# Loads begun a stage earlier, a shorter tables chain, and an edge softmax on 128 partitions

## The reference

```
x += gnn0(norm(x))   # three layers: batch-norm over the nodes, gather of the edges' source rows,
                     # degree-weighted sum by target, product with W (512x512), relu
x += ffn0(norm(x))   # each of 32 experts takes its 312 best tokens; up (512x1365), silu, down
                     # (one up matrix serves 4 experts), scatter-add weighted with the router's share
x += gnn1(norm(x))   # attention along edges: logits = q[rows].k[cols]/8 + edge_attr (8 heads)
                     # row_max = segment_max(logits, rows); p = exp(logits - row_max[rows])
                     # att = p / segment_sum(p, rows)[rows]; y = segment_sum(att * v[cols], rows)
x += ffn1(norm(x))   # two experts of 8 for each token, 512x32 each, gelu
```

## Time and profile before

| | |
|---|---|
| median of three runs | 3903.74 us (3902.39 to 3907.45) |
| the profiled execution's own time | 3906.87 us |
| its span, first to last instruction | 3905.1 us |
| mean granted TensorE clock | 0.886 of full speed |
| TensorE matmuls busy | 3254.1 us, 83% of the span |
| VectorE busy | 2462.7 us, 63% |
| ScalarE busy | 1388.0 us, 36% |
| GpSimd busy | 1235.2 us, 32% |

### The profile page before, as it was taken

The page is one execution under the profiler, slowest core; times in us unless marked ns, Lnnn a source line. Parts: engine busy times, 40 slices in busy tenths (PEclk is TensorE's granted clock), DMA queues, the critical chain, the costliest instruction groups (busy, mean ns, idle before and its releaser), DMA issues. The chain is left out here.

```text
span 3905.1 us, 61914 instructions
## 1 busy us (share of the span) xinstructions
PE 3254.1 (83%) x18334; PEld 2750.4 (70%) x18335; DVE 2462.7 (63%) x5844; ACT 1388.0 (36%) x2580; POOL 1235.2 (32%) x1606
## 2 busy tenths in 40 slices
PE   6845889997775309999999999999679992969999
PEld 1213667776774209999999999999668881856766
DVE  7855877644766764545455444454278877957776
ACT  4633655421112314445444444444211111114443
POOL 4752532222551012323222322323123320025552
PEclk9977999997555559999999999999889995989999
DMA  4313323335994034544444444444322111146663
GB/s 157 99 24 105 106 94 122 100 124 167 305 306 135 0 76 113 133 116 136 126 111 137 102 133 143 99 137 113 66 64 59 54 43 42 67 122 149 161 155 104
DMA packets 250361, 449.60 MB, mean 115 GB/s; under 512 B 65632, under 2 KB 71073, under 8 KB 249591
## 3 DMA queue, kind: packets, MB, share of 16 engines
q1 hardware_dynamic: 176425, 280.66, 22.0%
q0 software_dynamic: 62368, 145.38, 17.1%
q10 hardware_dynamic: 11318, 20.54, 1.4%
HBM read 319.38 MB, written 126.83 MB: 114 GB/s over the span
## 5 line engine op out<-in xcount | busy, mean ns | idle before, releaser
L1460 PE MATMUL experts_psU<-experts_x_hi,experts_up_hi 128*128 128x312 f32 (+1 forms) x1408 | 443.3, 315 | 22.9 <-issue 16.5
L1489 PE MATMUL experts_psY<-experts_hid_hi,experts_dn_hi 128*128 128x312 f32 (+1 forms) x1408 | 439.0, 312 | 0.0
L1461 PE MATMUL experts_psU<-experts_x_lo,experts_up_hi 128*128 128x312 f32 (+1 forms) x1408 | 436.8, 310 | 0.0
L1462 PE MATMUL experts_psU<-experts_x_hi,experts_up_lo 128*128 128x312 f32 (+1 forms) x1408 | 435.6, 309 | 0.0
L1490 PE MATMUL experts_psY<-experts_hid_lo,experts_dn_hi 128*128 128x312 f32 (+1 forms) x1408 | 431.3, 306 | 0.0
L1491 PE MATMUL experts_psY<-experts_hid_hi,experts_dn_lo 128*128 128x312 f32 (+1 forms) x1408 | 429.7, 305 | 0.0
L1419 POOL DMA_INDIRECT experts_xg<-xn,experts_token_i x96 | 123.4, 1285 | 663.0 <-DVE experts_token_i L1586 643.5
L1625 DVE TENSOR_TENSOR experts_hid_lo<-experts_hid,experts_hid_hi 128x312 fp32r<-128x312 f32 (+1 forms) x352 | 161.2, 480 | 252.2 <-ACT experts_hid L1552 252.2
L1550 ACT ACTIVATE experts_hid_hi<-experts_psU,experts_bup 128x312 fp32r<-128x312 f32 (+1 forms) x352 | 183.6, 522 | 322.1 <-PE experts_psU L1462 320.3
L1460 PEld LDWEIGHTS experts_psU<-experts_x_hi,experts_up_hi 128*128 128x128 f32 (+1 forms) x1408 | 265.2, 188 | 24.4 <-issue 22.0
L1617 DVE TENSOR_TENSOR experts_dn_lo<-experts_dn_raw,experts_dn_hi 128x1536 fp32r<-128x1536 f32 (+1 forms) x128 | 208.0, 1625 | 98.6 <-ACT experts_dn_hi L1528 98.4
(11 more groups left out here) (412 smaller groups left out, 8158.7 us busy)
## 6 DMA issues: line engine op xcount, KB each, us to landing
experts_dn_raw<-in_L_ffn_W_down SPq DMA_DIRECT2D x96, 768.0 KB, 4.6
conv<-gcn_diff SPq DMA_DIRECT2D x120, 256.0 KB, 2.9
experts_up_raw<-in_L_ffn_W_up SPq DMA_DIRECT2D x32, 682.5 KB, 8.4
index_xt<-in_x SPq DMA_DIRECT2D x78, 256.0 KB, 2.8
route_xt<-in_x SPq DMA_DIRECT2D x78, 256.0 KB, 4.9
x<-route_xt SPq DMA_DIRECT2D x78, 256.0 KB, 4.3
xn<-route_xn ACTq DMA_DIRECT2D x78, 256.0 KB, 5.0
two_xt<-x SPq DMA_DIRECT2D x78, 256.0 KB, 2.8
```

The costliest lines, as they stand in the source:

```text
L1460: pe.matmul(acc, up_hi[:, c, cols], x_hi[:, c, :], start=(c == 0), stop=False)
L1461: pe.matmul(acc, up_hi[:, c, cols], x_lo[:, c, :], start=False, stop=False)
L1462: mm = pe.matmul(acc, up_lo[:, c, cols], x_hi[:, c, :], start=False, stop=(c == C - 1))
L1489: pe.matmul(acc, dn_hi[0:w, m, cols], hid_hi[0:w, m, :], start=(m == 0), stop=False)
```

## The change

- `gcn_tables` loads edgeS and prevS (recS in place and one place back, 48-byte pieces) right behind prev; compares them into joinsS; and loads nextkey, the first key of each following tile, one on each of 40 partitions. link is computed from the transposed keys on 40 partitions x 128 (a row is a tile). The key broadcast comes in four pieces. The ten column sums go into one accumulator of 10 rows, each into its own row through a shifted one (one_row), followed by one copy and one subtraction. The moments, a0, c0 and the first four gathers of layer 0 move into this stage; `gcn_layer` skips them there. The stage now waits for the layers' weights, for the gathers and for edgeS and prevS.
- `slot_rows` gets a SyncE stream that loads the first up matrix into g.stage, a buffer of the outermost level; `experts` uses g.stage as up_raw, skips the load for the first expert, and at the end loads Wq and Wk into it.
- `attention_scores` loads only Wv and the three biases. It splits Wq and Wk first, Wv after the first tile is split; project waits for each matrix as it comes to it.
- `attention_weights` puts 16 tiles x 8 heads on 128 partitions, so three groups of 130 columns (128 edges and a column at each side) hold all 5120 edges x 8 heads. Each scan becomes: a scan of 3 x 130, its end values spread by a product and collected by a matmul into 8 x 40, a scan of these 40, handed out by a matmul and picked into the side column, and the same scan of 3 x 130 again. The keys of joinsS take the place of the load of rowsS.
- `top_two` issues its first four x tiles ahead of the weights.

The diff, cut to its core (lines without a sign are context):

```diff
@@ gcn_tables: SyncE
+            sp.dma_start(g.edgeS[:, :, :], g.recS[1:EP + 1, :].rearrange("(t p) c -> p t c", p=P)).then_inc(g.edges, 16)
+            sp.dma_start(prevS[:, :, :], g.recS[0:EP, :].rearrange("(t p) c -> p t c", p=P)).then_inc(g.edges, 16)
+            sp.wait_ge(cleared, 1)
+            sp.dma_start(nextkey[0:ET - 1, :], g.recD[1:EP + 1, :].rearrange("(t p) c -> t p c", p=P)[1:ET, 0, 0:1],
+                         allow_slow_non_contiguous=True).then_inc(following, 16)
             sp.wait_ge(copied, 1)
             sp.dma_start(g.rowsD[0, :].rearrange("(t p) -> t p", p=P), turned[:, :]).then_inc(stored, 16)
             sp.wait_ge(stored, 16)
-            sp.dma_start(key[:, 0:ET, :].rearrange("p t l -> p (t l)"), g.rowsD[0, :].partition_broadcast(P))\
-                .then_inc(rows, 16)
+            for k in range(ET // CH):
+                sp.dma_start(key[:, k * CH:(k + 1) * CH, :].rearrange("p t l -> p (t l)"),
+                             g.rowsD[0, k * CH * P:(k + 1) * CH * P].partition_broadcast(P)).then_inc(key_in[k], 16)
@@ gcn_tables: GpSimd
+        @block.gpsimd
+        def _(pool):
+            pool.wait_ge(loaded, 32)
+            for s in range(R):
+                pool.tensor_copy(idx[:, s, :], g.edgeD[:, ET - 1 - s, 1:2].bitcast(I32)).then_inc(staged, 1)
+                pool.wait_ge(staged, s + 1)
+                pool.sem_inc(waited, 1)
+                pool.indirect_dma_start(g.xt0[:, s, :], None, x, bass.IndirectOffsetOnAxis(ap=idx[:, s, :], axis=0))\
+                    .then_inc(g.gathered0[s], 16)
+            pool.wait_ge(moments, 1)
+            pool.tensor_tensor(rs[:, :], var[:, :], g.minus_half[:, 0:C], ALU.pow).then_inc(rooted_c, 1)
+            for s in range(R):
+                pool.wait_ge(g.gathered0[s], 16)
@@ gcn_tables: TensorE, sums of the weights
                 pe.wait_ge(weighed, (k + 1) * G)
-                if k >= 2:
-                    pe.wait_ge(low, k - 1)
-                pe.matmul(psW[0:1, k % 2, :], g.ones[:, 0:1],
-                          g.adj[:, k * G:(k + 1) * G, :].rearrange("p t l -> p (t l)"),
-                          start=True, stop=True).then_inc(summed, 1)
+                if k == 0:
+                    pe.wait_ge(one, 1)
+                mm = pe.matmul(psW[0:NG, :], one_row[:, NG - 1 - k:2 * NG - 1 - k],
+                               g.adj[:, k * G:(k + 1) * G, :].rearrange("p t l -> p (t l)"),
+                               start=(k == 0), stop=(k == NG - 1))
+            mm.then_inc(summed, 1)
@@ gcn_tables: ScalarE
-            for k in range(ET // G):
-                act.wait_ge(summed, k + 1)
-                act.copy(parts[:, 0, k * 512:(k + 1) * 512], psW[0:1, k % 2, :]).then_inc(high, 1)
+            act.wait_ge(summed, 1)
+            act.copy(parts[:, 0, :], psW[0:NG, :]).then_inc(high, 1)
@@ gcn_tables: VectorE
+            v.wait_ge(moved, 1)
+            step(v.tensor_scalar(g.mean0[:, :, :].rearrange("p k c -> p (k c)"), psS[:, 0:2 * C], 1.0 / g.N, None, ALU.mult))
+            step(v.tensor_tensor(sq[:, :], g.mean0[:, 0, :], g.mean0[:, 0, :], ALU.mult))
+            step(v.scalar_tensor_tensor(var[:, :], g.mean0[:, 1, :], EPS, sq[:, :], ALU.add, ALU.subtract))
+            v.sem_inc(moments, 1)
             v.wait_ge(loaded, 32)
             step(v.tensor_tensor(g.head[:, :], g.edgeD[:, :, 0], prev[:, :, 0], ALU.not_equal))
             step(v.scalar_tensor_tensor(g.head[:, :], g.edgeD[:, :, 0], float(g.N), g.head[:, :], ALU.is_lt, ALU.mult))
-            v.wait_ge(rows, 16)
-            v.tensor_tensor(link[:, :].rearrange("o (t l) -> o t l", l=P), key[0:1, 0:ET, :],
-                            key[0:1, 1:ET + 1, 0:1].to_broadcast([1, ET, P]), ALU.is_equal).then_inc(linked, 1)
+            v.wait_ge(copied, 1)
+            v.wait_ge(following, 16)
+            v.tensor_tensor(link[:, :], turned[:, :], nextkey[:, 0:1].to_broadcast([ET, P]), ALU.is_equal).then_inc(linked, 1)
+            step(v.memset(total[:, :], 0.0))
+            step(v.memset(square[:, :], 0.0))
             for t in range(ET):
+                if t % CH == 0:
+                    v.wait_ge(key_in[t // CH], 16)
                 v.tensor_scalar(g.adj[:, t, :], key[:, t, :], g.edgeD[:, t, 0:1], g.edgeD[:, t, 2:3],
                                 ALU.is_equal, ALU.mult).then_inc(weighed, 1)
-            for k in range(ET // G):
-                v.wait_ge(high, k + 1)
-                v.tensor_tensor(parts[:, 1, k * 512:(k + 1) * 512], psW[0:1, k % 2, :],
-                                parts[:, 0, k * 512:(k + 1) * 512].bitcast(F32), ALU.subtract).then_inc(low, 1)
+            v.wait_ge(g.edges, 32)
+            v.tensor_tensor(g.joinsS[:, :], g.edgeS[:, :, 0], prevS[:, :, 0], ALU.is_equal)
+            v.wait_ge(high, 1)
+            v.tensor_tensor(parts[:, 1, :], psW[0:NG, :], parts[:, 0, :].bitcast(F32), ALU.subtract).then_inc(low, 1)
+            v.wait_ge(rooted_c, 1)
+            v.wait_ge(g.gcn_weights, g.gcn_loads)
+            gb = g.gcn_gb[:, 0, :, :]
+            step(v.tensor_tensor(g.a0[:, :], rs[:, :], gb[:, 0, :], ALU.mult))
+            step(v.tensor_tensor(sq[:, :], g.mean0[:, 0, :], g.a0[:, :], ALU.mult))
+            step(v.tensor_tensor(g.c0[:, :], gb[:, 1, :], sq[:, :], ALU.subtract))
@@ slot_rows: SyncE
+            up_rows = W_up.rearrange("g h f -> (g h) f")
+            for c in range(g.D // P):
+                sp.dma_start(g.stage[:, c, :], up_rows[c * P:(c + 1) * P, :]).then_inc(g.up_loaded[c], 16)
+            for c in range(g.D // P):
+                sp.wait_ge(g.up_loaded[c], 16)
@@ experts: SyncE
-                if j == 0:
+                if j == 0 and not (isinstance(e, int) and e == 0):
...
+            sp.wait_ge(up_low, X // GR * C)
+            early = g.stage[:, :, :].rearrange("p c f -> p (c f)")[:, 0:2 * C * D].rearrange("p (n c d) -> p n c d", n=2, c=C)
+            for n in range(2):
+                sp.dma_start(early[:, n, :, :], w_next[n].rearrange("(c p) n -> p c n", p=P)).then_inc(g.w_early, 16)
+            sp.wait_ge(g.w_early, 32)
@@ attention_scores: SyncE
-            sp.dma_start(g.edgeS[:, :, :], g.recS[1:g.EP + 1, :].rearrange("(t p) c -> p t c", p=P)).then_inc(edges, 16)
+            sp.dma_start(raw[2], Wqkv[2].rearrange("(c p) n -> p c n", p=P)).then_inc(weights, 16)
             for n in range(3):
-                sp.dma_start(raw[:, n * C:(n + 1) * C, :], Wqkv[n].rearrange("(c p) n -> p c n", p=P)).then_inc(weights, 16)
                 sp.dma_start(bias[:, n, :], bqkv[n].partition_broadcast(P)).then_inc(weights, 16)
@@ attention_scores: ScalarE
-            act.wait_ge(weights, 96)
-            for n in range(3):
-                act.copy(w_hi[:, n, :, :], raw[:, n * C:(n + 1) * C, :]).then_inc(w_high, 1)
+            act.wait_ge(g.w_early, 32)
+            for n in range(2):
+                act.copy(w_hi[:, n, :, :], raw[n]).then_inc(w_high, 1)
 
             def heighten(t, j):
                 at_least(act, projected, t, 2, 3)
                 at_least(act, turned, t, 0, 2)
                 act.copy(x_hi[:, j, :, :], psT[:, :, :]).then_inc(high, 1)
+                if isinstance(t, int) and t == 0:
+                    act.wait_ge(weights, 64)
+                    act.copy(w_hi[:, 2, :, :], raw[2]).then_inc(w_high, 1)
@@ attention_scores: VectorE
-            v.wait_ge(weights, 96)
-            v.wait_ge(edges, 16)
-            for n in range(3):
+            v.wait_ge(g.edges, 32)
+
+            def lower_weights(n):
                 v.wait_ge(w_high, n + 1)
-                ins = v.tensor_tensor(w_lo[:, n, :, :], raw[:, n * C:(n + 1) * C, :], w_hi[:, n, :, :], ALU.subtract)
-            ins.then_inc(w_low, 1)
+                v.tensor_tensor(w_lo[:, n, :, :], raw[n], w_hi[:, n, :, :], ALU.subtract).then_inc(w_low, 1)
+            for n in range(2):
+                lower_weights(n)
...
             def lower(t, j):
                 at_least(v, high, t, 0)
                 v.tensor_tensor(x_lo[:, j, :, :], psT[:, :, :], x_hi[:, j, :, :], ALU.subtract).then_inc(low, 1)
+                if isinstance(t, int) and t == 0:
+                    lower_weights(2)
@@ attention_weights: TensorE
+            def collect(n):
+                pe.wait_ge(spread_out, n + 1)
+                pe.matmul(psK[0:H, 0:K * T], per_head[:, :], spread[:, :, :].rearrange("p k t -> p (k t)"),
+                          start=True, stop=True).then_inc(gathered, 1)
+
+            def hand_out(n, at):
+                pe.wait_ge(carried, n + 1)
+                pe.matmul(psR[:, 0:K * T], to_rows[:, :], state[:, at:at + K * T], start=True, stop=True)\
+                    .then_inc(spare, 1)
@@ attention_weights: VectorE
+            def spread_of(column):
+                step(v.tensor_tensor(spread[:, :, :], column.to_broadcast([P, K, T]),
+                                     per_tile[:, :].unsqueeze(1).to_broadcast([P, K, T]), ALU.mult))
+                v.sem_inc(spread_out, 1)
+
```

(31 more changed lines are left out.)

294 lines of the change are left out of this document (202 added, 92 removed).

## The result

The changed kernel takes 3818.86 us (median of 4 runs, 3814.86 to 3823.76) against 3905.16 for the one before beside it: ratio 0.9781, 95% interval 0.9767 to 0.9796, faster. In a second set of runs on another occasion it took 3814.34 (5 runs, 3811.51 to 3820.86), ratio 0.9776 (0.9763 to 0.9790). The forecast was 3817.

What follows compares the result with a forecast made beforehand. TensorE, busy 3254 of 3905 us, was taken to bound most of the run, serial-chain stages excepted. Gains 19.6 + 6.3 + 17.4 + 42.5 + 1 = 86.8 took 3906.9 to 3820.1; 3.1 above the median, so 3817, range 3799 to 3836.

Steps and rivals of the forecast that it cites:

- R5: Rival: the expert stage's granted clock falls from 0.99; at 0.93 the saving is gone, at 0.90 3949 us; chance 0.03.
- R4: Rival: early loads only move their wait; A, B and C yield 8 us instead of 43, time 3852; chance 0.04.
- A: Tables stage and start of layer 0: shorter chain and work moved forward gain 19.6 us, 13 to 25.
- B: Start of experts: the early first up matrix brings the first up product sooner, gain 6.3 us, 4 to 9.5.
- C: Scores stage: early Wq, Wk and edges bring the first stats sooner, gain 17.4 us, 14 to 19.
- R1: Rival: tables stage gains nothing, as small loads and gathers delay key, weights and stores; 10.8 us less, 3828; chance 0.12.
- R3: Rival: more comes free, first product of layer 0 and experts at their upper bounds; 3800 us, chance 0.06.
- A, tables: Tables stage: one subtraction replaces the one-partition chain of ten, small loads delay the key; gain 10.8 us.
- A, layer 0: Start of layer 0: no moment chain or first gather, stats 3.0 us after the start, not 11.8; gain 8.8.
- D: Edge softmax: short scans with carries replace four long scans, 72.3 us becomes 29.8; gain 42.5, 38 to 46.
- R2: Rival: edge softmax carries are dear, trips of 1.7 us; gain of D 29.5, time 3830; chance 0.08.
- E: Last stage, two experts: first four x tiles issued ahead of the weights; gain 1 us, -2.6 to +3.

Runs made afterwards that it cites:

- e5: Changed kernel with the load of nextkey issued behind the key's four pieces instead of ahead of the store of the turned keys: 3816.24 us, ratio 0.9775.
- e6: Changed kernel with edgeS and prevS loaded and compared in the slots stage instead of the tables stage: 3812.11 us, ratio 0.9764.
- e7: Changed kernel with the graph layers' weights, gammas, betas and biases loaded at the end of the index stage: 3810.65 us, ratio 0.9765.
- e3: Changed kernel with the first up matrix loaded in the experts stage again, as before: 3819.28 us, ratio 0.9795.
- e1: Changed kernel with the last stage's weights issued ahead of the x tiles again, as before: 3812.51 us, ratio 0.9766.
- e10: The changed kernel run again without edit, for a second profile: 3814.34 us, ratio 0.9776.
- e9: The kernel before run again without edit, for a second profile: 3902.18 us (one run).

## Why the prediction was right

The forecast of 3817 lies 1.9 us under the first median and 2.7 over the second. Step by step:

- **What bounds** held: the stages of serial chains gave the time, and the long stages of TensorE, experts and scores, kept theirs at 0.99 and 1.00 of the clock. So R5 did not come; but the ground given against it, that shorter gaps ahead of the experts had not lowered the clock in any row, was none, as the earlier trace rows hold no shorter gap. R4 (the loads only move their wait, 8 us in all) did not come: A, B and C gave 38.1. Nor did R1 (no gain in the tables stage) and R3 (3800).
- **A, tables: 10.8 forecast, 8.6 measured.** The key was forecast at 15.2 us after the stage's start and went at 16.4. The small loads were sized well: with nextkey behind the key (e5) it goes 5.3 us later than before, where 5.2 stood, and without them (e6) no later. The term that was mis-sized is nextkey, put at issues of 0.3 to 0.4 us: it took 3.24 us behind the small loads and cost the key 1.1. And the step "the parts' stores are last" failed: the landing of the weights, which is no term of the sum, came 41.7 us after the start, behind the last issue of the stores (39.9), and released the end; without the weights (e7) the stores end the stage, 3.2 to 4.2 us sooner. The signs set for A, the key compare at about 298 and the next stage at 321, stand for 18.5 and 41.5 us after the start; they came at 21.4 and 44.3. No run puts the parts of A back one by one: what each of them gives rests on the timelines. *The line rate that the Trainium skill gives in DMA: Bandwidth & Descriptors, Specifications, makes the two small loads 1.4 us together, as an estimate; its remark that transfers under 512 bytes miss that rate agrees with e6, where they cost about 5.*
- **A, layer 0: 8.8 forecast, 9.1 at its stats.** Of that 7.7 is left at the end of the three layers. At the start of layer 1 the changed kernel is still 9.3 us ahead, at the start of layer 2 7.7; the 1.6 us go with the granted clock of 0.84 in one stretch of layer 1, which six of the nine variants do not show.
- **B: 6.3 forecast, 5.8 measured** to the first product, of which e3 takes back 4.7 to 5.1; where the other 0.7 to 1.1 come from is not shown. The gather was taken to be awaited until 21.5 us after the stage's start and was until 22.9; the chain behind it took 7.5 us instead of 8.5.
- **C: 17.4 forecast, 16.0 measured.** First stats at 8.9 us after the start, where 7.5 was expected: VectorE, done with two splits, waits 1.78 us for the first gather. That term, 0.8 for the gathers, was too small. The 3.0 of the third split was near: from first stats to first product 14.1 us, 11.3 before, so 2.8.
- **D: 42.5 forecast, 44.3 measured.** Half of the difference is the stage before, taken as 72.3 us where the table has 73.2. Scans of 390 took the 0.97 read off the slope, the carry scan 0.23 for 0.24, the two trips of a pass 1.36 as forecast. Small operations of 48 columns took 0.21 and the set-up took 5.7 us where 0.26 and 6.4 stood. R2 (trips of 1.7) fell. *The errata section of the Trainium skill's VectorE: DVE Perf Modes speaks of a fixed cost for each small tile; the trace agrees (0.21 us for 48 columns), at a size nearer to the row of before than to the 0.11 that its table's formula gives as an estimate, and the cost of some 46 of them was far below what the long scans cost.*
- **E: 1 forecast; 0 within the spread** (e1, e10). The first profile alone would have read as a loss of 6.7.
- **Not forecast:** 2.3 us in the route, choose and slots stages, whose code is the same but for the new load, and 4.8 in the rest of the experts, as means of two profiles each. By e9 the first is spread, and most of the second follows the clock of the single execution. 3817 owes part of its nearness to them, and that part is luck: the forecast terms, as measured, add to 82.4 us (8.6 + 7.7 + 5.8 + 16.0 + 44.3), against 86.8 forecast.
- **Sums of the prediction that do not come out:** the lower bound of the tables stage's gain is 4.4 us and not 6 (10.8 less 5.2 and 1.2); eight trips of 1.7 us instead of 0.68 take 8.2 us from D and not the 13 of R2; layer 0 and experts at their upper bounds make 3813 and not the 3800 of R3; and the bounds of A to E, added as independent errors, give 3809 to 3827 and not 3804 to 3831. The forecast itself does not rest on them.

## What to carry to other kernels

In these runs the time of a scan went by its columns and not by its partitions: 0.23 us for 8x40, 0.97 for 128x390, 10.81 for 8x5120, about 2.1 ns a column. So a segmented scan on 8 rows could be cut into tiles on 128 with carries; the carries were priced by a trip read elsewhere in the same trace (0.68 us), and the stage came out within 2 us. A load moved ahead of others on one queue put back what stood behind it: the edges by source cost 5 us in the tables stage, while the slots stage, whose queue is idle, took them and the up matrix, 3.3 MB, at its old length of 33.8 us. And when a load is moved back, look at what stands behind its user on the engine: in e5 40 compares waited for a value that they did not need.
